# Attention and mixture-of-experts kernel on one core: three reorderings in the head of the program

## What is computed

```python
x = x + xattn(ctx, layernorm(x), Wq)        # per sequence: softmax(causal(q k^T / sqrt(d))) v, with k = v = ctx Wq^T
f = layernorm(x)                            # second norm
gates = softmax(f @ gate_W); top 2 of 8, renormalised to cw
out = f
for e in range(8):
    out = out + cw[:, e:e+1] * (relu(f @ W1[e] + b1[e]) @ W2[e] + b2[e])
x = x + out
```

## Time and profile before

| | |
|---|---|
| Time, median of 3 runs | 130.19 us (129.76 to 130.45) |
| The profiled execution's own time | 129.6 us |
| Its span, first to last instruction | 127.8 us |
| PE busy | 120.1 us (94%) |
| DVE busy | 105.1 us (82%) |
| ACT busy | 93.7 us (73%) |
| POOL busy | 53.5 us (42%) |
| Granted TensorE clock | 1.0 throughout |

### The profile page before, as it was taken

The page is one execution under the profiler, slowest core; times in us unless marked ns, Lnnn a source line. Parts: engine busy times, 40 slices in busy tenths (PEclk is TensorE's granted clock), DMA queues, the critical chain, the costliest instruction groups (busy, mean ns, idle before and its releaser), DMA issues. The chain is left out here.

```text
span 127.8 us, 3279 instructions
## 1 busy us (share of the span) xinstructions
PE 120.1 (94%) x1175; PEld 90.6 (71%) x1175; DVE 105.1 (82%) x399; ACT 93.7 (73%) x193; POOL 53.5 (42%) x57
## 2 busy tenths in 40 slices
PE   6987899999979999999999999999999989999991
PEld 2584686677758768778769778778776757776690
DVE  0629899889999999968998999958998799666682
ACT  4348477998778936995789947993799377989830
POOL 7199253330194860330286640330459303445400
PEclk9999999999999999999999999999999999999999
DMA  2999920000000000200000001000000002000002
GB/s 65 322 282 328 291 57 8 0 0 0 5 0 0 5 3 0 82 5 0 0 0 5 0 0 60 25 5 0 3 0 8 0 0 87 0 3 5 0 0 82
DMA packets 9904, 5.54 MB, mean 43 GB/s; under 512 B 504, under 2 KB 9888, under 8 KB 9888
## 3 DMA queue, kind: packets, MB, share of 16 engines
q1 hardware_dynamic: 9744, 5.27, 15.2%
q10 hardware_dynamic: 144, 0.07, 0.2%
HBM read 4.28 MB, written 1.05 MB: 42 GB/s over the span
## 5 line engine op out<-in xcount | busy, mean ns | idle before, releaser
L693 POOL TENSOR_TENSOR h_lo<-h,h_hi 128x512 f16<-128x512 f32 x24 | 28.7, 1197 | 39.7 <-ACT h L571 39.3
L571 ACT ACTIVATE h<-psH,b1T 128x512 f32<-128x512 f32 x64 | 43.4, 690 | 0.2 <-PE psH L386 0.2
L570 ACT ACTIVATE h_hi<-psH,b1T 128x512 f16<-128x512 f32 x48 | 33.0, 688 | 11.8 <-PE psH L386 11.8
L867 DVE SCALAR_TENSOR_TENSOR acc<-psY,weight_y,acc 128x128 f32<-128x128 f32 x125 | 35.1, 342 | 1.4 <-PE psY L407 1.2
L382 PE MATMUL psH<-x_hi,w_hi 128*128 128x512 f16 x62 | 23.5, 380 | 0.8 <-ACT h L571 0.8
L851 DVE TENSOR_TENSOR h_lo<-h,h_hi 128x512 f16<-128x512 f32 x24 | 16.5, 690 | 9.2 <-ACT h L571 9.0
L386 PE MATMUL psH<-x_lo,w_hi 128*128 128x512 f16 x62 | 23.5, 379 | 0.0
L383 PE MATMUL psH<-x_hi,w_lo 128*128 128x512 f16 x62 | 23.5, 379 | 0.0
L407 PE MATMUL psY<-w_hi,h_hi 128*128 128x128 f16 x192 | 22.7, 219 | 0.0
L407 PE MATMUL psY<-w_lo,h_hi 128*128 128x128 f16 x192 | 22.7, 219 | 0.0
L407 PEld LDWEIGHTS psY<-w_hi,h_hi 128*128 128x128 f16 x192 | 15.3, 98 | 2.2
(11 more groups left out here) (187 smaller groups left out, 185.7 us busy)
## 6 DMA issues: line engine op xcount, KB each, us to landing
w_sb<-in_L_ffn_W_dram SPq DMA_DIRECT2D x8, 256.0 KB, 4.4
out_dram<-acc SPq DMA_DIRECT2D x3, 256.0 KB, 2.3
x_sb<-in_x_dram SPq DMA_DIRECT2D x2, 256.0 KB, 4.2
ctx_sb<-in_ctx_dram SPq DMA_DIRECT2D x2, 256.0 KB, 4.6
x_sb<-in_x_dram SPq DMA_DIRECT2D x1, 512.0 KB, 6.6
ctx_sb<-in_ctx_dram SPq DMA_DIRECT2D x1, 512.0 KB, 7.7
out_dram<-acc SPq DMA_DIRECT2D x2, 128.0 KB, 1.8
wq_sb<-in_L_xattn_Wq_dram ACTq DMA_DIRECT2D x1, 64.0 KB, 2.7
```

The source lines that it names most:

```text
L570: nc.scalar.activation(h_hi[:, C * (e % 2) + c, :], psH[c][:, :], ACT.Relu, bias=bias, scale=scale)
L571: nc.scalar.activation(h[:, C * (e % 2) + c, :], psH[c][:, :], ACT.Relu, bias=bias, scale=scale).then_inc(h_ready, 1)
L693: nc.gpsimd.tensor_tensor(h_lo[:, i, :], h[:, i, :], h_hi[:, i, :], ALU.subtract).then_inc(hlo0_ready, 1)
L867: last = nc.vector.scalar_tensor_tensor(out=o, in0=y, scalar=weight_y[:, g % 2, t, e:e + 1], in1=o, op0=ALU.mult, op1=ALU.add)
```

## The change

Two places of the written order change, and no instruction is added or removed.

On DVE, `mean_and_var` of group 1 moves from behind `second_norm` to ahead of it, and `small_lo_parts` moves from ahead of `second_norm` to between the two `x_lo_part` of group 0. On ACT, `values_out` of group 1 moves from behind `x_hi_part` to behind the first ReLU. The wait for `b1_ready` moves too, to stand directly ahead of that ReLU.

```diff
@@ scalar
             for ts, banks in HALVES:
                 x_hi_part(0, ts, banks)
-            values_out(1, ALL, FIRST_BANKS)
-            act.wait_ge(b1_ready, 1)
             w1_hi_part(2)
             w2_hi_part(2)
+            act.wait_ge(b1_ready, 1)
             hidden_relu(0, 0)
+            values_out(1, ALL, FIRST_BANKS)
             gate_exps(0)
@@ vector
             for ts, banks in HALVES:
                 second_variance(0, ts, chain)
+            mean_and_var(TG, 2 * TG, chain)
+            for ts, banks in HALVES:
+                second_norm(0, ts)
+            x_lo_part(0, *HALVES[0])
             small_lo_parts()
-            for ts, banks in HALVES:
-                second_norm(0, ts)
-            mean_and_var(TG, 2 * TG, chain)
-            for ts, banks in HALVES:
-                x_lo_part(0, ts, banks)
+            x_lo_part(0, *HALVES[1])
             w2_lo_part(0)
```

More of the change, by code:

```diff
@@ L990, in _ @@
                 second_variance(0, ts, chain)
-            small_lo_parts()
+            mean_and_var(TG, 2 * TG, chain)
             for ts, banks in HALVES:
                 second_norm(0, ts)
-            mean_and_var(TG, 2 * TG, chain)
-            for ts, banks in HALVES:
-                x_lo_part(0, ts, banks)
+            x_lo_part(0, *HALVES[0])
+            small_lo_parts()
+            x_lo_part(0, *HALVES[1])
             w2_lo_part(0)
```

## The result

The changed kernel took 130.80 us (median of 20 runs, 130.00 to 131.21), the kernel before, run beside it, 129.88 us (129.08 to 130.61). The ratio is 1.0076, with a 95% interval of 1.0056 to 1.0096: slower by 0.99 us (0.73 to 1.25). The prediction was +0.86 us; its 131.05 us stood on a median of three runs of before that was 0.3 us above the median of twenty. So the forecast time owes part of its fit to luck: its base was 0.3 us too high and its rise about 0.1 us too small. The rise is what the prediction is to be judged by.

A forecast was written before the change was run, and what follows sets the result against it. PE was taken as the bound, paced in the head by the second x_lo's chain. Terms 0 + 0 + 0.86 + 0 = +0.86 us, against the 130.19 us median, gave 131.05 us; range 130.3 to 131.5.

The forecast's parts named there:

- The chain of the head: POOL's power, xf, transposes, second x_hi, second x_lo, below, gate_exps, exponentials, PE at 25.6 us; x_lo's delay sets the time.
- The statistics, cost 0: Group 1's mean and variance ahead of xf: 0.64 us covered by POOL's second power, second half of xf stays at 16.65.
- `base_sum` at 17.6: On POOL, base_sum follows the earlier first_rstd(1) at 17.6 us rather than 18.93; by itself this brings nothing.
- The small lower parts: On DVE, gate_lo comes up at 17.88 us, is held by base_sum to 18.71 and ends at 18.84.
- (a): Not held: gate_lo starts before base_sum, or its narrow float16 write is not held; +0.1, 130.3 us; chance 0.14.
- `b_cat` and the second `x_lo`: On DVE, b_cat ends at 19.12, second x_lo starts 19.04 to 19.12 against 18.22: +0.82 to +0.90, taken as +0.86.
- The upper bound: POOL's power up to 0.27 longer, base_sum just before gate_lo, hold 0.27 longer: +1.13 to +1.17 us.
- PE's 0.6 us ahead of the second products: PE waits for the second x_lo before the second hidden products, losing some 0.6 us, inside the 0.86.
- The values, cost 0: ACT's values behind the first ReLU fill the idle 0.67 us ahead of gate_exps; uncovered, up to 0.59 us.
- The rule of who is held: DVE instructions with two SBUF operands and wide POOL elementwise ones exclude each other; PSUM operands and POOL's powers are exempt.
- (b): Faster: second x_lo before 18.22 carries the exponentials along, up to 0.6 us of PE's waits; 129.6 us; chance 0.04.
- (c): Moves bring and cost nothing: the hold exists, but PE makes it up at stalls after 26 us; 130.4 us; chance 0.07.

The follow-up runs named there:

- e4: Kernel before, with w1's low part for experts 2 and 3 moved from ahead of gate_top into the gates' choice; 129.19 against 129.93 us, ratio 0.9965.
- e11: Kernel before with only the statistics moved, plus two tiny DVE memsets at its start; one execution, no ratio, second x_lo 3.25 us behind the last variance.
- e3: Changed kernel, with POOL's base_sum of group 0 waiting until the first low part of w2 is written; ratio 1.0013.
- e7: Changed kernel, with base_sum split in two halves, the second waiting for the first low part of w2; ratio 1.0021.
- e8: Changed kernel, with base_sum's addition run once more ahead of it, into a tile that the first ReLU overwrites; ratio 1.0147.
- e12: Changed kernel with base_sum waiting for w2's first low part, and b_cat ahead of gate_lo; one execution, second x_lo 3.10 us behind the last variance.
- e2: Kernel before with only ACT's part of the change; ratio 0.9994.
- e6: Kernel before with only the small lower parts moved between the two x_hi/x_lo steps' x_lo; statistics stay behind second_norm; ratio 1.0020.
- e10: Kernel before with the statistics ahead of the small lower parts, and both ahead of second_norm; ratio 1.0056.
- e5: Kernel before with only the statistics of group 1 moved, between the small lower parts and second_norm; ratio 1.0041.
- e9: Kernel before with only the statistics moved, executed once more for its profile; no ratio, second x_lo 3.68 us behind the last variance.

## Why the prediction was right

- **The chain of the head** was right. A delay of 0.95 us at the second `x_lo` came out as 0.95 at `below`, at `gate_exps` and at PE's output product, and 0.91 at the end. e4 shows the same for a gain, up to PE's own limit.
- **The statistics, cost 0** was right in the changed kernel: the second half of `xf` stands at 1.34 us in both. The cover was POOL's power. In e11 the small parts lie under it too, and the second half of `xf` stands at 1.68: the 0.34 us that the cover could not hold.
- **`base_sum` at 17.6**, that is 2.29 us behind the variance: measured 2.24.
- **The small lower parts**, the term that decided: `gate_lo` was to come up at 2.57 and end at 3.53. Measured 2.58 and 3.53. That it is narrow and writes float16 did not save it, against the second leg of rival (a). e3, e7 and e8 show that it is `base_sum` that holds it.
- **`b_cat` and the second `x_lo`**: +0.82 to +0.90, taken in the middle, measured +0.95. The upper value was the right one to take (e12), and each held instruction adds another 0.01 to 0.04 us behind the end of its predecessor, which no term had. This is what the sum was short of: 0.86 against 0.95. The upper bound has the same looseness: +1.13 adds 0.27 to the middle value and not to the lower one, which gives +1.09. Nothing hangs on it.
- **PE's 0.6 us ahead of the second products**: the weight load was idle 0.74 us and PE 0.46. It lay inside the 0.95, as said.
- **The values, cost 0** was right (e2: 0.9994). What the prediction did not say is where ACT's hole would go.
- **The rule of who is held** was right for two operands in SBUF and for an operand in PSUM, but it was drawn too narrowly. `xf`, with one tensor input in SBUF and its output there, is held too. Two of group 2 in the kernel before take 1.44 us beside POOL's `h_lo`, where two alone took 0.60:

```profile
65.38 1.44 DVE L787 TENSOR_SCALAR xf<-x,mv,rstd 128x128 f32<-128x128 f32 x2
65.54 1.19 POOL L693 TENSOR_TENSOR h_lo<-h,h_hi 128x512 f16<-128x512 f32 x1
```

  In the head this changed nothing, since `xf` runs beside POOL's powers there.
- **The rivals.** (a) would have needed `gate_lo` to come up ahead of `base_sum`; e6 is that case, at 1.002, for another reason (late statistics keep POOL busy with its power). (b) is what e4 does by another edit, and it brought 0.39 us at the end of the span, not the 0.6 that (b) had. (c), whose 130.4 us came with no working, did not occur: 0.91 of 0.95 us arrive at the end.

In short, neither of DVE's two moves alone put `gate_lo` beside `base_sum`: the second `x_lo` came 0.36 us late with the small parts alone (e6) and 0.34 with the statistics alone and no gap (e11). Both together cost it 0.16 us with the collision away (e3); what the change cost beyond that comes from their having put an instruction of 0.17 us behind one of 1.27.

## What to carry to other kernels

When an edit brings GpSimd work forward, list which VectorE instructions it will now run beside. In these traces two kinds were held behind a wide GpSimd instruction: those with two operands in SBUF, however small, and a TENSOR_SCALAR from SBUF to SBUF (`xf`, and `weight_cat` of L840, 1.04 us instead of 0.20 at 105.95 us in the kernel before). Those with an operand in PSUM and the statistics of the norms (0.28 us each) ran beside it at their usual length, and GpSimd's powers of 2 and 4 columns held nobody. The one that starts second pays until the other is nearly done. Idle time that the profile puts down to a semaphore deserves a look at the other engine's row: where it ends as a GpSimd instruction ends, the semaphore may not be the cause. And a chain of waits found for a loss can be pulled the other way: to move off it work that nobody needs yet brought 0.39 us (e4), while filling ACT's idle time brought nothing (e2).

## What the runs showed that was not expected

- Executions of one program differ by up to 1.5 us (129.08 to 130.61 for before), and in the profiles this lies ahead of the last variance of group 0, which stands between 14.84 and 16.24 us. What lies behind it repeats: from the output product of expert 1 to the end of the span it is 101.95 to 102.01 us in 13 of the 14 profiles. In e2 it is 102.53, by the lost race of group 2. Distances from a fixed instruction told 0.1 us where times needed 12 runs for 0.3%.
- A gap of 0.52 us (0.30 in e10) ahead of one DVE instruction that nothing in the profile explains, repeatable in e5 and e9 and gone when two memsets stand ahead of it. It made e5 and e10 0.3 to 0.4 us slower than their sums.
- The race in e6 between a DVE instruction and POOL's `base_sum` was decided by 0.01 us, in favour of DVE. What it looks like when POOL wins such a race is in e2's trace, in group 2: the DVE instruction is held for 1.13 us. Two such races stand in the loop of every kernel here, so part of the spread of the times may come from them; that was not measured.
